# Feed-forward first pass: x rounded to bf16 on GpSimd and transposed by a DMA for seven of eight groups, in place of TensorE transposes and copies out of PSUM

## The reference

```python
def _quant_per_tensor(x):
    scale = jnp.maximum(jnp.max(jnp.abs(x)), MIN_RANGE) / QP      # QP = 127
    return (_ste_round(x / scale), scale)

def _qlinear(x2d, w, b):
    xq, sx = _quant_per_tensor(x2d)
    wq, sw = _quant_per_tensor(w)
    out = jnp.matmul(xq, wq.T) + b[None, :]
    return out * (sw * sx)

h = _qlinear(x.reshape(-1, D), w1, b1)        # 8192 x 256 by 256 x 1024
h = jax.nn.gelu(h, approximate=False)
o = _qlinear(h, w2, b2)                       # 8192 x 1024 by 1024 x 256
...
x = x + _L0_ffn_ref(_layernorm(x, axis=-1), L0_ffn_w1, L0_ffn_b1, L0_ffn_w2, L0_ffn_b2)
```

## Time and profile before

| what | us |
|---|---|
| median of 3 runs | 1664.6 |
| profiled execution | 1667.77 |
| its span | 1666.0 |
| first unit's gelu starts (first pass) | 1475.55 |
| last maximum over a unit is taken, next VectorE instruction starts | 1557.37 |

### The profile page before, as it was taken

The page is one execution under the profiler, slowest core; times in us unless marked ns, Lnnn a source line. Parts: engine busy times, 40 slices in busy tenths (PEclk is TensorE's granted clock), DMA queues, the critical chain, the costliest instruction groups (busy, mean ns, idle before and its releaser), DMA issues.

```text
span 1666.0 us, 52582 instructions
## 1 busy us (share of the span) xinstructions
PE 1554.7 (93%) x16058; PEld 1245.2 (75%) x16058; DVE 1468.4 (88%) x6202; ACT 1223.2 (73%) x2511; POOL 1062.8 (64%) x1168
## 2 busy tenths in 40 slices
PE   6689999999999999999999999999999999678898
PEld 5568888888888888888888888888888887544465
DVE  3779999999999999999999999999999996679876
ACT  4767777777777777777777777777777776479875
POOL 3467777777777777777777777777777777621000
PEclk9789999999999999999999999999999999889999
DMA  6000000000000000000000000000100000221154
GB/s 212 1 18 29 28 28 28 28 28 28 23 27 28 28 28 28 28 28 28 28 24 24 23 27 28 28 25 26 28 28 28 28 28 17 89 89 51 58 181 167
DMA packets 77734, 71.03 MB, mean 43 GB/s; under 512 B 6272, under 2 KB 77184, under 8 KB 77696
## 3 DMA queue, kind: packets, MB, share of 16 engines
q1 hardware_dynamic: 76736, 70.41, 13.3%
q10 hardware_dynamic: 960, 0.13, 0.1%
HBM read 45.36 MB, written 25.17 MB: 42 GB/s over the span
## 4 chain that ended last, share of the span: by engine, by line
PE 39%; DVE 34%; issue 12%; ACT 7%; DMA 4%; POOL 2%; DVEq 1%; SPq 1%; ACTq 0%; POOLq 0%
PE banks L124 10%; PE banks L127 8%; PE banks L128 7%; DVE scores L1379 6%; DMA x_in<-in_x_dram 3%; DVE tile_max L2110 3%; DVE sparse_in L1450 2%; DVE heads_t_half L1401 2%; DVE xn L1334 2%; PE banks L926 2%; PE banks L906 2%; DVE left L1431 2%; PE banks L798 2%; PE banks L2001 2%; DVE g_t_half L1355 2%
## 5 line engine op out<-in xcount | busy, mean ns | idle before, releaser
L646 POOL TENSOR_TENSOR shifted<-scores,score_max 128x512 f32<-128x512 f32 x256 | 266.8, 1047 | 200.2 <-DVE score_max L1379 195.5
L652 POOL TENSOR_TENSOR exp_t<-exp_copy,exp_t 128x512 f16<-128x512 f32 x256 | 303.9, 1187 | 81.2 <-ACT exp_copy L1168 78.7
L1379 DVE CUSTOM_DVE_ANT_0 scores<-banks,mask 128x128 f32<-128x128 f32 x1024 | 232.6, 284 | 6.5 <-PE banks L906 2.9
L638 POOL TENSOR_TENSOR v_nat<-kv_copy,v_nat 128x512 f16<-128x512 f32 x128 | 149.3, 1166 | 44.5 <-ACT kv_copy L1146 44.5
L1143 ACT ACTIVATE q_t<-banks 128x512 f16<-128x512 f32 x128 | 77.1, 603 | 131.4 <-PE banks L128 131.1
L926 PE MATMUL banks<-ident,shifted 128*128 128x128 f32 x1024 | 153.6, 278 | 9.4 <-ACT exp_copy L1168 6.1
L1166 ACT ACTIVATE exp_t<-banks 128x512 f16<-128x512 f32 x256 | 152.4, 595 | 5.7 <-PE banks L116 2.9
L1168 ACT ACTIVATE exp_copy<-banks 128x512 f32<-128x512 f32 x256 | 155.1, 606 | 0.0
L1146 ACT ACTIVATE kv_copy<-banks 128x512 f32<-128x512 f32 x252 | 149.9, 595 | 0.0
L638 POOL TENSOR_TENSOR k_t<-kv_copy,k_t 128x512 f16<-128x512 f32 x124 | 144.1, 1162 | 0.0
L114 PE MATMUL banks<-v_nat,exp_t 128*128 128x66 f16 x1024 | 121.9, 195 | 7.6 <-POOL exp_t L652 3.2
(11 more groups left out here) (275 smaller groups left out, 5160.6 us busy)
## 6 DMA issues: line engine op xcount, KB each, us to landing
x_in<-in_x_dram SPq DMA_DIRECT2D x32, 256.0 KB, 2.8
ctx_in<-in_ctx_dram SPq DMA_DIRECT2D x32, 256.0 KB, 2.7
x_residual<-x SPq DMA_DIRECT2D x64, 128.0 KB, 1.7
x_normalised<-normed SPq DMA_DIRECT2D x32, 256.0 KB, 2.2
shared<-x_normalised SPq DMA_DIRECT2D x8, 1024.0 KB, 5.3
shared<-x_residual SPq DMA_DIRECT2D x16, 512.0 KB, 3.7
out_dram<-shared SPq DMA_DIRECT2D x16, 512.0 KB, 3.1
mask<-in_fside_Bx1xSxS_dram SPq DMA_DIRECT2D x64, 64.0 KB, 2.1
```

The costliest lines, as they stand in the source:

```text
L638: pool.tensor_tensor(hilo(dst, *at)[LO], src, hilo(dst, *at)[HI], ALU.subtract).then_inc(kv_split, 1)
L646: pool.tensor_tensor(shifted[:, q % 2], scores[:, q % 2], score_max[:, q % 2, :].unsqueeze(2).to_broadcast([P, QUAD, P]), ALU.subtract).th ...
L652: pool.tensor_tensor(exp_t[:, q % 2, LO], exp_copy[:, q % 2], exp_t[:, q % 2, HI], ALU.subtract).then_inc(exp_split, 1)
L1379: op = dve.tensor_tensor_reduce(scores[:, q % 2, h, :], sc_bank(q)[:, tile(h)], mask[:, b, :], 1.0, NEG, ALU.add, ALU.max, score_max[:, q ...
```

## The change

Group 0 goes as before, only its place in `xq_t` is laid out otherwise. For groups 1 to 7 GpSimd does two instructions of 128x2048: it scales and adds MAGIC in place, then subtracts MAGIC and writes bf16 into one of two new buffers `xq_nat` (`NAT`), which lie in a part of `shared` that was free in the first pass. Before the second instruction it waits for the transpose of two groups before. SyncE then issues one DMA transpose for the group, 128 x 2048 bf16 in and 16 blocks of 128x128 out, straight into `xq_t`, whose order becomes block, feature half, token. Between these it issues the loads of group g+3 behind the transpose of group g. The transpose of group g from 4 on waits for the units of group g-4. TensorE waits once per group for the DMA. The 112 transposes of TensorE for these groups, and the 14 copies each of VectorE and ScalarE, are gone.

```diff
-    xq_t = sb("xq_t", [P, KEPT, DT, TOK], BF16)
+    NAT = 2
+    xq_nat = shared[:, SLOTS * GB * D:SLOTS * GB * D + NAT * GB * D // 2].bitcast(BF16).rearrange("p (n c) -> p n c", n=NAT)
+    xq_t = sb("xq_t", [P, KEPT, GB, DT, P], BF16)
...
+    def wait_turned(eng, g):
+        eng.wait_ge(x_turned[g % NAT], 16 * ((g - 1) // NAT + 1))
...
     def sync(sp):
-        for g in range(SLOTS, GROUPS):
-            sp.wait_ge(xt_full, PARTS * (g - SLOTS) + PARTS)
-            sp.dma_start(x_load[:, g % SLOTS, :].rearrange("p (b d) -> p b d", b=GB),
-                         normed_groups[g]).then_inc(loaded[g % SLOTS], 16)
+        def load_next(g):
+            if g < GROUPS:
+                sp.dma_start(x_load[:, g % SLOTS, :].rearrange("p (b d) -> p b d", b=GB),
+                             normed_groups[g]).then_inc(loaded[g % SLOTS], 16)
+
+        def turn(g):
+            sp.wait_ge(x_rounded, g)
+            if g >= KEPT:
+                sp.wait_ge(u_full, (g - KEPT + 1) * ET)
+            sp.dma_start_transpose(xq_t[:, g % KEPT].rearrange("p b t s -> p (b t) s"),
+                                   xq_nat[:, g % NAT, :]).then_inc(x_turned[g % NAT], 16)
+
+        sp.wait_ge(xt_full, PARTS)
+        load_next(SLOTS)
+        for g in range(1, GROUPS):
+            turn(g)
+            load_next(g + SLOTS)
...
-        sp.wait_ge(xt_full, PARTS * GROUPS)
         sp.wait_ge(b2_ready, 3)
...
         def round_x(g):
             pool.wait_ge(loaded[g % SLOTS], 16 * (g // SLOTS + 1))
-            for h in range(2):
-                at = slice(h * GB * D // 2, (h + 1) * GB * D // 2)
-                pool.tensor_scalar(x_load[:, g % SLOTS, at], x_load[:, g % SLOTS, at], inv_scale[:, 0:1], MAGIC,
-                                   ALU.mult, ALU.add).then_inc(rounded_pool, 1)
+            pool.tensor_scalar(x_load[:, g % SLOTS, :], x_load[:, g % SLOTS, :], inv_scale[:, 0:1], MAGIC,
+                               ALU.mult, ALU.add).then_inc(rounded_pool, 1)
+            if g > NAT:
+                wait_turned(pool, g - NAT)
+            pool.wait_ge(rounded_pool, g)
+            pool.tensor_scalar(xq_nat[:, g % NAT, :], x_load[:, g % SLOTS, :], -MAGIC, 1.0,
+                               ALU.add, ALU.mult).then_inc(x_rounded, 1)
...
         for g in range(GROUPS):
-            for h in (PARTS - 2, PARTS - 1):
-                wait_part(pe, g, h)
+            if g == 0:
+                for h in (PARTS - 2, PARTS - 1):
+                    wait_part(pe, h)
+            else:
+                wait_turned(pe, g)
             for t in range(ET):
                 n = g * ET + t
                 if n >= U1:
                     pe.wait_ge(h_ready, n - U1 + 1)
                 hidden_unit(u1_bank(n), g, t, u_full)
-                if t in AFTER and g + 1 < GROUPS:
-                    x_transpose(g + 1, AFTER.index(t))
...
# scalar (the same in vector, for parts 0 and 2)
-                if t in (AFTER[1], AFTER[3]) and g + 1 < GROUPS:
-                    take_x(g + 1, AFTER.index(t))
```

More of the change, by code:

```diff
@@ L1718, in feed_forward @@
     PART = TOK // PARTS
-    AFTER = (0, 1, 3, 4)
     HB = GB // 2
@@ L1757, in feed_forward @@
     xt_full, xt_act, xt_dve = sem("xt_full"), sem("xt_act"), sem("xt_dve")
+    x_rounded, x_turned = sem("x_rounded"), [sem(f"x_turned{n}") for n in range(NAT)]
     u_full, h_ready, h_seen = sem("u_full"), sem("h_ready"), sem("h_seen")
@@ L1773, in feed_forward, with wait_part, first_part @@
     acc_bank = lambda half, b: psum[:, 4 + 2 * half + b // 2, :]
-    part_of = lambda g, h: g * (PARTS // 2) + h // 2 + 1
-    def wait_part(eng, g, h):
-        eng.wait_ge((xt_dve, xt_act)[h % 2], part_of(g, h))
+    def wait_part(eng, h):
+        eng.wait_ge((xt_dve, xt_act)[h % 2], h // 2 + 1)
+    def wait_turned(eng, g):
+        eng.wait_ge(x_turned[g % NAT], 16 * ((g - 1) // NAT + 1))
+    def first_part(h):
+        return (xq_t[:, 0, 2 * h:2 * h + 2].rearrange("p b t s -> p t b s"),
+                xt_bank(h).rearrange("p (t b s) -> p t b s", t=DT, b=2))
     on_act = lambda k, t: t % 3 != 2 if again(k) else t // 2 % 2 == 1
@@ L1941, in round_x @@
             pool.wait_ge(loaded[g % SLOTS], 16 * (g // SLOTS + 1))
-            for h in range(2):
-                at = slice(h * GB * D // 2, (h + 1) * GB * D // 2)
-                pool.tensor_scalar(x_load[:, g % SLOTS, at], x_load[:, g % SLOTS, at], inv_scale[:, 0:1], MAGIC,
-                                   ALU.mult, ALU.add).then_inc(rounded_pool, 1)
+            pool.tensor_scalar(x_load[:, g % SLOTS, :], x_load[:, g % SLOTS, :], inv_scale[:, 0:1], MAGIC,
[5 more added lines that the diff above has]
+                               ALU.add, ALU.mult).then_inc(x_rounded, 1)
         pool.wait_ge(scales_done, 1)
-        round_x(1)
-        for g in range(2, GROUPS):
+        for g in range(1, GROUPS):
             round_x(g)
@@ L1954, in tensor, with x_transpose @@
         ident = keep["ident"][:]
[L1956 to L1960, removed]
+        def x_transpose(h):
+            pe.wait_ge(rounded_dve, h // 2 + 1)
             if h >= 2:
-                wait_part(pe, g, h - 2)
-            elif g > 0:
-                wait_part(pe, g - 1, h + 2)
+                wait_part(pe, h - 2)
             for dt in range(DT):
@@ L1968, in x_transpose @@
                     mm = pe.transpose(xt_bank(h)[:, (2 * dt + b) * P:(2 * dt + b + 1) * P],
-                                      x_load[:, g % SLOTS, at:at + P], ident)
+                                      x_load[:, 0, at:at + P], ident)
             mm.then_inc(xt_full, 1)
@@ L1975, in hidden_unit @@
                     mm = pe.matmul(bank[:, half * HALF:(half + 1) * HALF], keep["w1_q"][:, kt, t * P:(t + 1) * P],
-                                   xq_t[:, g % KEPT, kt, half * HALF:(half + 1) * HALF],
+                                   xq_t[:, g % KEPT, half * HB:(half + 1) * HB, kt, :],
                                    start=(kt == 0), stop=(kt == DT - 1))
@@ L1980, in tensor @@
         for h in range(PARTS):
-            x_transpose(0, h)
+            x_transpose(h)
         for g in range(GROUPS):
-            for h in (PARTS - 2, PARTS - 1):
-                wait_part(pe, g, h)
+            if g == 0:
[3 more added lines that the diff above has]
+                wait_turned(pe, g)
             for t in range(ET):
@@ L2028, in gelu @@
             act.activation(out, src, ACT.Gelu, bias=b1_scaled[:, t:t + 1], scale=both[:, 0:1]).then_inc(ready, 1)
[L2030 to L2035, removed]
         for h in (1, 3):
-            take_x(0, h)
+            act.wait_ge(xt_full, h + 1)
+            dst, src = first_part(h)
+            act.activation(dst, src, ACT.Copy, bias=-MAGIC).then_inc(xt_act, 1)
         act.wait_ge(scales_done, 1)
@@ L2094, in vector @@
         dve.tensor_scalar(b1_scaled[:], keep["b1_col"][:], both[:, 0:1], None, ALU.mult).then_inc(scales_done, 1)
[L2096 to L2102, removed]
         for h in (0, 2):
-            take_x(0, h)
+            dve.wait_ge(xt_full, h + 1)
+            dst, src = first_part(h)
+            dve.tensor_scalar(dst, src, MAGIC, None, ALU.subtract).then_inc(xt_dve, 1)
         for g in range(GROUPS):
@@ L2111, in vector @@
                                   apply_absolute_value=True).then_inc(h_seen, 1)
-                if t in (AFTER[0], AFTER[2]) and g + 1 < GROUPS:
-                    take_x(g + 1, AFTER.index(t))
         dve.wait_ge(h_seen, UNITS)
```

## The result

The changed kernel has a median of 1655.79 us over 5 runs (1654.72 to 1657.15), the kernel before 1664.25 us over 5 (1663.56 to 1667.19). The ratio is 0.9946, 95% interval 0.9934 to 0.9957: 8.5 us less. The profiled execution took 1657.15 us, its span 1655.3.

A forecast was written before the change was run, and what follows sets the result against it. The prediction took VectorE's instruction stream as the bound; its 14 copies of 0.60 us gave 8.4 us and everything else nothing, so 1664.6 - 8.4 = 1656.2 us, range 1654.5 to 1668 (1654.5 to 1658.5 for this case alone).

The forecast's parts named there:

- The bound: First pass: VectorE's gapless stream, 64 maxima of 1.127 us plus 14 copies of 0.60; removing the copies gains 8.4 us.
- ScalarE's copies: First pass: removing ScalarE's 14 copies gains nothing by itself; had they stayed, ScalarE would be the bound at 78 us.
- TensorE: First pass: removing 112 transposes gains nothing; work falls to 0.86 of every 1.127 us, at the full clock.
- rival 3: First pass: TensorE's clock falls to its lower level, 1.61 us per unit, 31 us more, 1687; chance 0.04.
- The clock step of the argument: TensorE: after a 2.25 us gap the clock is granted 0.50, so each such gap costs its length and 1.3 us more.
- The sum: Whole kernel: 8.4 us of VectorE's stream go, turn and second pass keep their order; 1664.6 - 8.4 = 1656.2 us.
- The layout of `xq_t`: TensorE's moving operand becomes four runs of 128 columns; taken as costing nothing, bounded by 0.27 us slack per unit.
- GpSimd: Groups 1 to 7: two instructions of 2.2 us each, 4.4 of 9.0 us per group, hidden; group 1's bf16 about 1475.0.
- The DMA transpose: SyncE's queue: 3.1 us taken per transpose, behind the load whose data are there at 1479.15; group 1 at about 1482.
- the deadline: Group 1 of the first pass: its x must be there by 1483.4, a slack of 4.2 us after the load's data.
- Rival 1: Group 1: first transpose lands late, 5.9 us at 46 ns per packet; 1659.1, up to 1668; chance 0.13.
- Rival 2: First pass: transposes of T each set the pace, ending it at 1503.7 + 7T; slower from T = 7.7 us; chance 0.16.

The follow-up runs named there:

- e2_act_copies: The changed kernel with 14 copies of 128x512 out of PSUM put back on ScalarE alone; 1662.50 us, ratio 0.9990 to the kernel before.
- e3_pe_transposes: The changed kernel with 112 f32 transposes of 128x128, read by nobody, put back on TensorE; 1655.87 us, ratio 0.9949 to the kernel before.
- e5_transpose_on_act: The changed kernel with the seven DMA transposes issued by ScalarE instead of SyncE, loads still by SyncE; 1665.88 us, ratio 1.0009 to the kernel before.
- e11_load_first: The changed kernel with SyncE waiting until its previously issued load has landed before issuing each transpose; 1656.42 us, ratio 0.9947 to the kernel before.

## Why the prediction was right

**The bound.** It held in full: 64 x 1.127 + 14 x 0.60 before, 64 x 1.127 after, and with the 14 copies put back on VectorE the time is 1663.61 against the 1664.2 expected. The pass lost 8.35 us and the median 8.46, against 8.4; the interval of the ratio leaves 7.2 to 11.0 us, so that the median agrees to 0.1 is more than the runs can tell.

**ScalarE's copies** gained nothing by themselves and would have been the bound had they stayed: shown by `e2_act_copies`, at 77.4 us of pass where 78 had been written. The 78 took 0.6 us per copy from its duration; between starts one costs 0.48 us there (1474.37 to 1474.85).

**TensorE** had room for its transposes and for the lighter pace, at a granted clock of 1.00 from 1480 to 1540; rival 3 is out. The clock step of the argument was too firm: the gap of 2.25 us before gave 0.50 and one of 2.35 us after did not. A gap of some 2.3 us cost the level in four of the twelve traces that have it, and not in the other eight; what decides it is not shown. The sum took the turn as unchanged, and in the profiled pair it is not.

**The layout of `xq_t`**: 64 matmuls in 16.57 us, 1.04 per unit with ScalarE setting the pace, no stall. What a unit costs TensorE itself is seen where other work follows it at once: 0.86 us from start to start in `e3_pe_transposes` (1474.49 to 1475.35), as in the kernel before (1474.43 to 1475.29). Nothing, as taken.

**GpSimd**: 1.98 and 1.90 us per instruction of 2048 columns, a little under the 2.2 taken. The bf16 tile of group 1 stood at 1473.3.

**The DMA transpose** is the term that was mis-sized: 8.3 us to landing in the kernel as it runs, 7.2 for the first, where 3.1 had been taken; by itself it takes 3.8. My sum put load and transpose one behind the other. In the trace they run side by side and both get longer (the load's median goes from 5.3 to 7.0 us), as sharing the engines would have it. The two errors cancelled, and that is luck: the sum had group 1 land 1482.25 - 1476.79 = 5.5 us after the first maximum, and it landed 1480.6 - 1475.65 = 4.9 us after it. By the argument of the prediction the deadline was 1482.3 in this execution, so 1.7 us were to spare.

Rival 1 failed by its duration. The page of the changed kernel has 91296 packets in q1 where the earlier trace rows had 76736, so a transpose has 2080, close to the 2048 that were counted; but the average price of 46 ns per packet does not hold for them. With no load in flight, in `e5_transpose_on_act` from 1511.9 to 1513.4, they move 290 GB/s, so the 0.52 MB take about 1.8 us and not 5.9. Rival 2's formula fails because it adds loads and times to landing one behind the other: with T = 8.3 it ends the pass at 1503.7 + 7 x 8.3 = 1561.8, and it ended at 1547.9; it sent doubled transposes to 1697, and they took 1658.68. The trace is near the 261 GB/s that the Trainium skill gives in "DMA: Bandwidth & Descriptors" (Latency and other measured facts), with 290 GB/s while the data flow and 3.8 us to landing. It speaks against reading the 1309 ns per block of the Trainium skill's "VectorE: DVE Perf Modes" (The three transpose paths) as a serial price: 16 blocks land in 3.8 us.

**Where the profiled pair misleads.** Its two executions differ by 10.6 us. The pass explains 8.35; the turn went from 2.5 to 1.6 us by the clock, and the first maximum came 1.1 us earlier, a start that lies anywhere from 1473.1 to 1476.9 in the traces of kernels with the same work ahead of it.

## What to carry to other kernels

When an engine's stream has no gap, price an edit by the distance between starts in that stream, and check the engine that is next: here both engines' copies had to go for the full gain. Before work is moved to a DMA, ask for its time beside the loads that run with it and for what covers the first one; here a steady stream had 2 of 9 us to spare, the first group none. The engine that issued a DMA transpose was held 1.3 to 6.8 us for it here, so the transpose belongs on an engine with nothing else to do.

## What was not expected of the hardware

A transpose of 128x2048 bf16 in SBUF holds the issuing engine 1.3 to 2.0 us and lands in 3.6 to 3.9 with no load ahead of it (`e11_load_first`). Right behind a 1 MB load on the same queue these are 5.1 to 6.5 and 7.2 to 9.5 us; beside 3 MB of loads from another queue they were 6.1 and 14.0. A plain load holds it 0.4 to 0.6 us. Identity transposes in TensorE's gaps, 24 in 2.78 us, kept the granted clock at 1.00 where it was 0.50.
